# Last feed-forward of an eight-stage block: input normalised inside the first attention layer, gated sum and store inside the last gated layer

## The reference, cut to what matters

```python
def _layernorm(x, axis=-1, eps=1e-05):
    m = jnp.mean(x, axis=axis, keepdims=True)
    v = jnp.var(x, axis=axis, keepdims=True)
    return (x - m) / jnp.sqrt(v + eps)

# in _L3_ffn_ref: DEPTH = 2, HEADS = 8, DIM_HEAD = 64, WINDOW = 64, HID = 341
def _layer(x, wqkv, qs, ksc, wo, lg, lb, w1, b1, w2, b2):
    h = shift_token(x)
    q, k, v = jnp.split(h @ wqkv, 3, axis=-1)      # then by heads
    q = l2norm(q) * qs
    k = l2norm(k) * ksc
    q, k = rotary_xpos(q, k)
    o = local_attention(q, k, v)
    x = x + o @ wo
    h = shift_token(x)
    h = (h - mu) / jnp.sqrt(var + 1e-05) * lg + lb
    a, g = jnp.split(h @ w1 + b1, 2, axis=-1)
    x = x + (a * jax.nn.gelu(g, approximate=False)) @ w2 + b2
    return x
for l in range(DEPTH):
    x = _layer(x, wqkv[l], ...)

x = x + jnp.tanh(g_ffn[3]) * _L3_ffn_ref(_layernorm(x, axis=-1), ...)
return x
```

## Time and profile before

| | |
|---|---|
| median of 3 runs | 3924.22 us (3916.47 to 3931.73) |
| the profiled execution's own time | 3918.53 us |
| its span, first to last instruction | 3916.6 us |
| PE busy in the span | 3314.0 us (85%) |
| DVE busy | 2456.6 us (63%) |
| ACT busy | 1686.4 us (43%) |
| POOL busy | 1167.3 us (30%) |
| mean granted TensorE clock | 0.919 of full |

### The profile page before, as it was taken

How to read it: one execution, slowest core, us unless ns; L and a number is a source line. 1 busy time by engine, 2 the same in 40 slices (tenths; PEclk the granted TensorE clock), 3 DMA queues, 4 the chain that set the end, 5 groups by cost and what they waited for, 6 DMA issues and landing times. The chain is left out here.

```text
span 3916.6 us, 89814 instructions
## 1 busy us (share of the span) xinstructions
PE 3314.0 (85%) x31371; PEld 2123.4 (54%) x31371; DVE 2456.6 (63%) x5197; ACT 1686.4 (43%) x3144; POOL 1167.3 (30%) x1454
## 2 busy tenths in 40 slices
PE   3687999999688795589949997499999779999976
PEld 1464445444566542466646664266666446666644
DVE  7666111111688779878866676777776547777654
ACT  1333222222577536555512223266665226666522
POOL 1664000000233100044410003077775107777510
PEclk8766999999899897799959998799999899999988
DMA  4211000000000005011100002100000110000011
GB/s 131 59 40 51 0 0 0 0 0 0 17 13 13 4 16 226 16 54 45 32 17 1 0 0 74 53 10 9 9 9 4 35 32 10 9 9 9 4 35 56
DMA packets 163476, 107.80 MB, mean 28 GB/s; under 512 B 91390, under 2 KB 151980, under 8 KB 162348
## 3 DMA queue, kind: packets, MB, share of 16 engines
q1 hardware_dynamic: 161788, 104.02, 9.1%
q10 hardware_dynamic: 1584, 2.44, 0.2%
HBM read 68.52 MB, written 16.78 MB: 22 GB/s over the span
## 5 line engine op out<-in xcount | busy, mean ns | idle before, releaser
L2265 POOL TENSOR_TENSOR la_turned<-la_turned,la_sines 128x1024 f32<-128x1024 f32 x128 | 301.7, 2357 | 143.3 <-DVE la_sines L2191 143.3
L908 DVE TENSOR_TENSOR l0f_y<-A,l0f_s 128x512 f32<-128x512 f32 x16 | 11.1, 692 | 463.4 <-PE A L850 463.4
L2259 POOL TENSOR_TENSOR la_scaled<-la_turned,la_rlen 128x1024 f32<-128x1024 f32 x128 | 243.6, 1903 | 16.9 <-POOL la_rlen L2252 13.5
L1175 POOL COPY l1x_vd<-half 128x16 f32<-128x16 f32 x8 | 1.2, 212 | 605.8 <-POOLq L48 605.8
L2161 ACT ACTIVATE la_sq<-A 128x1024 f32<-128x1024 f32 x128 | 131.2, 1025 | 108.1 <-PE A L2311 81.6
L2183 DVE TENSOR_TENSOR la_turned<-A,la_cos 128x1024 f32<-128x1024 f32 x128 | 155.5, 1215 | 29.7 <-issue 15.4
L2145 ACT ACTIVATE la_prob<-la_prob 128x512 f32<-128x512 f32 x128 | 80.7, 630 | 204.1 <-DVE la_prob L2204 204.1
L2499 ACT ACTIVATE gg_gate<-B,gg_b 128x512 f32<-128x512 f32 (+1 forms) x96 | 65.9, 686 | 211.0 <-PE B L2525 211.0
L2201 DVE TENSOR_REDUCE la_top<-B 128x8 f32<-128x512 f32 x128 | 88.6, 692 | 108.4 <-PE B L2324 108.4
L2196 DVE TENSOR_REDUCE la_length<-la_sq 128x16 f32<-128x1024 f32 x128 | 155.1, 1212 | 0.0
L2331 PE MATMUL B<-la_wo,la_oT 128*128 128x128 f32 x1024 | 150.1, 290 | 2.7 <-ACT la_oT L2141 2.7
(11 more groups left out here) (444 smaller groups left out, 9085.8 us busy)
## 6 DMA issues: line engine op xcount, KB each, us to landing
l1f_spill<-l1f_work SPq DMA_DIRECT2D x16, 768.0 KB, 3.2
l1f_xT<-l1f_spill SPq DMA_DIRECT2D x16, 768.0 KB, 6.1
l2x_ctx<-in_ctx SPq DMA_DIRECT2D x128, 64.0 KB, 2.2
memory_vd<-vd SPq DMA_DIRECT2D x64, 68.0 KB
X<-in_x SPq DMA_DIRECT2D x4, 1024.0 KB, 6.5
gates_rows<-in_ctx_rows SPq DMA_DIRECT2D x16, 256.0 KB, 2.8
memory_ctxT<-in_ctxT SPq DMA_DIRECT2D x64, 64.0 KB, 1.9
l1x_ctxT<-in_ctxT SPq DMA_DIRECT2D x64, 64.0 KB
```

The costliest lines, as they stand in the source:

```text
L2259: pool.tensor_tensor(by_head(scaled), by_head(turned), spread_heads(rlen[j % 2][:], W3), ALU.mult)\
L2265: pool.tensor_tensor(turned[j % 2][:], turned[j % 2][:], sines[j % 2][:], ALU.add)\
```

## The change

Three things are done.

- The stage `l3f_in` is gone. Layer 0 of `local_attention` normalises the tiles itself: four of them ahead of the loop, the others one for each step, eight tiles ahead of the step's own (`norm_y`, at the end of VectorE's step). SyncE's copy of a tile waits for the new counter `normed_y`.
- The stages `l3f_out` and `store` are gone. In layer 1 of `gated_gelu` VectorE scales `w2` (with the bias row in it) by `tanh(g)` once; GpSimd adds `y * tanh(g)` to `X`, chunk by chunk, in two instructions after its power; and `add` puts the contraction's result onto `X` and not onto `y`.
- SyncE stores each chunk of `X` as soon as it is added (256 KB each), and the stage ends when all 16 are there. For this the loop of SyncE in `gated_gelu` is written as steps, in both layers.

```diff
-def steps4(eng, step, quads=QUADS):
+def steps4(eng, step, quads=QUADS, last=1):
...
-    with eng.Fori(1, quads - 1) as it:
+    with eng.Fori(1, quads - last) as it:
...
-    for it in (quads - 1, quads):
+    for it in range(quads - last, quads + 1):
...
@@ local_attention
+        normed_y, inputs_seen = st.counter("normed_y", BEFORE), st.sem("inputs_seen")
...
                 def shift_in(it, j):
                     t = it * 4 + j
                     sp.wait_ge(h_turned, done(it, j, 4))
+                    if layer == 0:
+                        sp.sem_inc(inputs_seen, 1)
+                        sp.wait_ge(normed_y, done(it, j))
+                        sp.sem_inc(inputs_seen, 1)
...
+                def norm_y(it, j):
+                    t = it * 4 + j
+                    normed(dve, m, y[:, t, :], t).then_inc(normed_y, 1)
+
                 for j in range(4):
                     dve.memset(hs[j][:], 0.0).then_inc(ones_set, 1)
                     dve.memset(vd[j][:, :, :, W3:W3 + 1], 1.0).then_inc(ones_set, 1)
+                if layer == 0:
+                    for j in range(4):
+                        norm_y(0, j)
...
                     at4(it, j, -1, outputs)
-
-                steps4(dve, step)
+                    if layer == 0:
+                        at4(it, j, 8, norm_y)
+
+                steps4(dve, step, last=2)
@@ gated_gelu
+        last_layer = layer == 1
...
+                def store(it, j):
+                    tiles = bass.ds(it * 8 + 4 * j, TPC)
+                    sp.wait_ge(added[j], past(it + 1))
+                    sp.sem_inc(seen, 1)
+                    sp.dma_start(d["out"][:, tiles, :], m.X[:, tiles, :]).then_inc(stored, 16)
+
+                def step(it, j):
+                    at(it, j, 2, shift_in, CHUNK_PAIRS)
+                    if last_layer:
+                        at(it, j, -2, store, CHUNK_PAIRS)
...
                 def add(it, j):
                     dve.wait_ge(down[j], past(it + 1))
-                    ty = y[:, bass.ds(it * 8 + 4 * j, TPC), :]
+                    if last_layer:
+                        dve.wait_ge(based[j], past(it + 1))
+                    ty = (m.X if last_layer else y)[:, bass.ds(it * 8 + 4 * j, TPC), :]
...
+                if last_layer:
+                    for k, o in ((P, slice(0, F - 1)), (last_k + 1, slice(F - 1, F))):
+                        dve.tensor_scalar(w2[0:k, o], w2[0:k, o], m.tanh_g[0:k, 7:8], None, ALU.mult).then_inc(w2_gated, 1)
...
                         pool.tensor_tensor(rstd[j][:], var[j][:], half_power[:], ALU.pow).then_inc(rooted[j], 1)
+                        if last_layer:
+                            tiles = bass.ds(it * 8 + 4 * j, TPC)
+                            pool.wait_ge(based[j], past(it))
+                            pool.tensor_tensor(gated_y[j][:], y[:, tiles, :],
+                                               m.tanh_g[:, 7:8, None].broadcast_to([P, TPC, P]), ALU.mult)\
+                                .then_inc(y_scaled[j], 1)
+                            pool.wait_ge(y_scaled[j], past(it + 1))
+                            pool.sem_inc(pool_seen, 1)
+                            pool.tensor_tensor(m.X[:, tiles, :], m.X[:, tiles, :], gated_y[j][:], ALU.add)\
+                                .then_inc(based[j], 1)
...
                 pe.wait_ge(loaded, 16 * len(loads))
+                if last_layer:
+                    pe.wait_ge(w2_gated, 2)
@@ l3_ffn, program
-    with Stage(nc, "l3f_in") as st:
-    ...
-    with Stage(nc, "l3f_out") as st:
-    ...
-        store(nc, m, d)
```

More of the change, by code:

```diff
@@ L2398, in gated_gelu @@
         h_in = [st.sem(f"h_in{j}") for j in range(2)]
+        last_layer = layer == 1
+        seen, pool_seen = st.sem("seen"), st.sem("pool_seen")
+        if last_layer:
+            gated_y = st.two("gated_y", [P, TPC, P])
+            w2_gated, stored = st.sem("w2_gated"), st.sem("stored")
+            y_scaled, based = st.sem2("y_scaled"), st.sem2("based")
         (stat, parts, terms, aggregated, rooted, normed_h, turned, copied, up, gelued, hidden, down, added) = (
@@ L2411, in _, with shift_in @@
                 sp.wait_ge(zeroed, 2)
-                with sp.Fori(0, CHUNK_PAIRS) as it:
-                    for j in range(2):
-                        ty = y[:, bass.ds(it * 8 + 4 * j, TPC), :]
[L2415 to L2418, removed]
+                def shift_in(it, j):
+                    ty = y[:, bass.ds(it * 8 + 4 * j, TPC), :]
+                    sp.wait_ge(normed_h[j], past(it))
+                    sp.sem_inc(seen, 1)
+                    sp.dma_start(hs[j][:, :, 0:S], ty[:, :, 0:S]).then_inc(h_in[j], 16)
+                    for b in range(0, P, S):
+                        sp.dma_start(hs[j][b + 1:b + S, :, S:P], ty[b:b + S - 1, :, S:P]).then_inc(h_in[j], 16)
+                def store(it, j):
+                    tiles = bass.ds(it * 8 + 4 * j, TPC)
+                    sp.wait_ge(added[j], past(it + 1))
+                    sp.sem_inc(seen, 1)
+                    sp.dma_start(d["out"][:, tiles, :], m.X[:, tiles, :]).then_inc(stored, 16)
[3 more added lines that the diff above has]
+                        at(it, j, -2, store, CHUNK_PAIRS)
+                steps(sp, step, CHUNK_PAIRS)
+                if last_layer:
+                    sp.wait_ge(stored, 16 * NCH)
             @block.vector
@@ L2597, in __init__ @@
         self.B = [ctx.enter_context(nc.psum_tensor(f"B{j}", [P, 1024], F32)) for j in range(2)]
[L2600 to L2607, removed]
 def program(nc, d, stages=None):
```

## The result

The changed kernel takes 3878.85 us (median of 4 runs, 3877.30 to 3892.97), the kernel before 3920.34 us on the same chip; ratio 0.9899, 95% interval 0.9865 to 0.9932. Two later comparisons of the same kernel gave 0.9908 (0.9890 to 0.9926) and 0.9894 (0.9878 to 0.9911). The profiled execution took 3878.28 us.

A forecast was written before the change was run, and what follows sets the result against it. It took TensorE to bound the attention loop, with VectorE alone at the last feed-forward's start and 24.3 us without overlap at the end. Terms of -19.7, -21.4, +0.8, +7.6 gave 3885.8 us; forecast 3889, 3880 to 3897 (full range 3875 to 3905).

The forecast's parts named there:

- Start, -19.7: Before the first attention: it begins behind the reciprocal, not the last normalisation, saving 19.7 us (bounds 18.5 to 20).
- Attention loop, 0: First attention: the moved normalisations cost 0, covered by VectorE's idle 0.75 us; bounds 0 and 0.2 us per tile.
- rival E: First attention: normalisation held behind GpSimd's scaling every tile; slower than before, 3924 to 3930 us or over 3990; chance 0.04.
- End, -21.4: After the last add: only a hand-over and a 256 KB store's landing remain, 24.3 us falling to 2.9.
- Scaling w2, 0: Start of last gated layer: two VectorE instructions, under 1 us, hidden in the wait for y's first copy; 0.
- The added wait, +0.8: Last gated loop: the add's extra wait costs 0.05 us, 16 times, +0.8 us; bounds 0 and 2.9.
- GpSimd beside the normalisation, +7.6: Last gated loop: GpSimd's two instructions hold normalisations; 0.43 us in each of 14 chunks, 1.6 in chunk 0; +7.6 us.
- The sum, -32.7: Whole kernel: -19.7 - 21.4 + 0.8 + 7.6 = -32.7 us, giving 3885.8 for an execution like the profiled one.
- Rival B: Last gated layer hides all of GpSimd's added work; gain 40.3 us, 3878 to 3884; chance 0.20.
- C: Last gated layer: GpSimd becomes the bound, each chunk 1.3 us late; gain 20.5 us, 3898 to 3904; chance 0.15.
- D: Attention loop pays 0.2 us per tile through delayed GpSimd rotation and scaling; 12.8 us less gain, 3899 to 3904; chance 0.11.

The follow-up runs named there:

- front_only: Changed kernel keeping the normalisation moved into the first attention, with the gated sum and one store put back as before; 3898.93 us, 0.9937 of the kernel before.
- The two later places: Changed kernel with the first attention's norm_y between shift and add, or between add and lengths; the attention's 63 steps took 487.9 and 478.3 us.
- behind_norm: Changed kernel with GpSimd waiting for the chunk's normalisation before its two last-gated-layer instructions; 3879.85 us, in a second comparison 3881.12 us (0.9893 of the kernel before).
- norm_in_rotation: Changed kernel with the first attention's norm_y between the shift and the add, during GpSimd's rotation; the attention's 63 steps took 487.9 us.
- norm_before_shift: Changed kernel with the first attention's norm_y between the sine terms and the shift; the attention's 63 steps took 464.0 us.

## Why the prediction was right, and where a term was off

- *Start, -19.7:* measured -19.57, in `front_only` the same. Right, with its cover: the four early normalisations are done 0.1 us before the first load is issued.
- *Attention loop, 0:* 464.0 against 464.8 us. Right, and for the reason given: VectorE's wait shrank from 0.75 to 0.49. The cover is narrower than the prediction had it, though: rival E's price for a hold behind the scaling assumed that only `make_qk` and the scores wait. The two later places show `mix` and `turn_o` waiting too: a hold of 1.06 us ahead of the `add` costs 0.38 us for each tile, one of 0.88 behind it 0.23, where I would have said nothing. And a tile takes 464.8 / 63 = 7.38 us in the kernel before, not the 7.45 that the count of instructions in a window gave.
- *End, -21.4:* measured -21.17, but two errors cancel. The last store lands 2.02 us after its issue, as 14 of the 16 do, where I had taken 2.8; and from its landing to the span's end are 1.04 us in which the stage is closed, for which I had nothing. (The fit that the prediction takes from the Trainium skill, "DMA: Bandwidth & Descriptors", section on the anatomy of one DMA, is stated there for transfers that GpSimd issues, and these come from SyncE: its 2.6 us for 256 KB are 0.6 too long.)
- *Scaling w2, 0:* right. The two instructions end 5.4 us after the layer's first load, and the first statistics begin 7.17 us after it, with them (`behind_norm`) and without (`front_only`).
- *The added wait, +0.8:* measured 0. In `behind_norm` the adds lie exactly as before.
- *GpSimd beside the normalisation, +7.6:* the mechanism held to the instruction: one is held behind the first (0.07 us), one behind the second (1.0), the four are 1.07 late (I said 1.1). The size was too large: a step is 0.34 longer and not 0.43 (9.89 and 9.99 us, where I had named 10.1 to 10.2 as the sign), so the slack comes out as 1.07 - 0.34 = 0.73 and not 0.67, over some 13 chunks and not 14, 4.4 us. At the start the four take 2.83 us and not 1.11, 1.72 late where I said 1.6. Of this only 1.36 shows against the kernel before, because something that I had left out pays 0.36 back: with SyncE's loop written as steps the first three copies are issued closer together, and in `front_only`, where GpSimd has nothing to add, the first transposes come 11.42 us behind the first load and not 11.78. Together 5.7.
- *The sum, -32.7:* the terms as measured give -35.0. The three comparisons of this kernel show 41.5, 32.5 and 40.3 us between the medians. In the first the profiled execution of the changed kernel ran 4.07 us shorter ahead of the last reciprocal and 1.0 between the first load of the attention and that of the last gated layer; what is left is not explained. The forecast was 3889, with 3880 to 3897 about it, and 3878.85 came 10 us below: 2.3 of them are the terms above, the rest is that scatter and the 3.2 that I had added because the medians before lay above the profiled execution. So the terms are borne out, and where in the range the median fell is chance.

Rival B's time came closest in the first comparison, but not its mechanism: the gated layer did pay. C, D and E did not happen, and `norm_in_rotation` shows a mild form of E. In `norm_before_shift` the hold of 0.65 us at the scaling's end cost nothing; one of E's full 1.9 us was not tried.

## What to carry to other kernels

A serial head or tail of one engine is worth its full length, to be read from two rows, the last before it and the first after it; what its work costs inside a loop depends on where in the queue it stands. When work goes to GpSimd, look at which VectorE instructions it will run beside and which of them it holds (here the normalisations, not what reads PSUM and not the reduction), and let GpSimd wait until they are through, if it has the time: one wait gave back all that was lost here. Below half a per cent compare stretches of the profile, since the medians carry the scatter of every other stage.

## What was not expected of the hardware

A VectorE normalisation (one SBUF tensor in and out, 128x128, 0.34 us) issued while GpSimd runs an instruction on SBUF ends with that one: 1.4 to 1.6 us in a rotation of 2.35, 0.99 beside a scaling. Sums, products and reductions with an operand in PSUM, and the length reduction of 1.21 us, keep their time in the same places. (The Trainium skill, "GPSIMD Engine Reference", Key points, names two-port modes and two SBUF inputs as what contends. The second agrees with the statistics held in `behind_norm`, 1.26 us for 0.16; for the first, no trace here shows the mode in which the normalisation runs.)

The seven stages ahead of the last feed-forward vary by several microseconds from one execution to the next at the same code: to the last reciprocal's end 2498.0, 2499.6 and 2509.8 us in three executions of the changed kernel. The fifth and sixth of them take 729 us together in every trace, so the spread lies in the others. The cause was not looked for.
